# A two-layer kernel with a routed expert stage: expert units of 128 rows in place of 256, four result buffers, one PSUM bank per block, and the transposed rows copied by VectorE

## The reference

```python
P = softmax(xn @ Wg)                       # 8 experts
_, topk_idx = top_k(P, 2)                  # two experts for each token
P_norm = P * mask / (sum(P * mask) + EPS)
h   = gelu(einsum('bsd,edf->ebsf', xn, W1) + b1)   # 128 -> 512
y_e = einsum('ebsf,efd->ebsd', h, W2) + b2         # 512 -> 128
y   = einsum('ebsd,bse->bsd', y_e, P_norm)
x   = x + s * silu(y)
```

## Time and profile before

| | us |
|---|---|
| three runs | 524.37, 519.02, 523.99; median 523.99 |
| profiled execution, its time | 523.02 |
| profiled execution, span of its instructions | 521.3 |

### The profile page before, as it was taken

The page is one execution under the profiler, slowest core; times in us unless marked ns, Lnnn a source line. Parts: engine busy times, 40 slices in busy tenths (PEclk is TensorE's granted clock), DMA queues, the critical chain, the costliest instruction groups (busy, mean ns, idle before and its releaser), DMA issues.

```text
span 521.3 us, 10243 instructions
## 1 busy us (share of the span) xinstructions
PE 460.1 (88%) x3176; PEld 392.3 (75%) x3176; DVE 291.8 (56%) x1056; ACT 215.9 (41%) x528; POOL 165.6 (32%) x251
## 2 busy tenths in 40 slices
PE   3868979999999999999998898999999999999633
PEld 2556867987888978879877687788888888888511
DVE  6687976947785848576666843133233333333327
ACT  3354436453563445432444220244444444444412
POOL 8601002304223151334314140033444444444500
PEclk9996979979999999999998987799999999999958
DMA  7799000000000010000001031011222222222177
GB/s 196 236 269 159 10 1 20 22 1 22 21 17 27 1 36 7 22 22 22 22 6 36 6 109 51 1 52 51 58 67 56 67 61 62 62 62 61 51 262 232
DMA packets 37173, 33.22 MB, mean 64 GB/s; under 512 B 5381, under 2 KB 29833, under 8 KB 37129
## 3 DMA queue, kind: packets, MB, share of 16 engines
q1 hardware_dynamic: 32432, 23.66, 17.9%
q0 software_dynamic: 4352, 8.99, 5.1%
q10 hardware_dynamic: 344, 0.03, 0.0%
HBM read 17.32 MB, written 15.34 MB: 63 GB/s over the span
## 4 chain that ended last, share of the span: by engine, by line
PE 80%; DVE 6%; issue 5%; ACT 5%; DMA 2%; SPq 0%; ACTq 0%; DVEq 0%; POOL 0%; POOLq 0%
PE psA L901 14%; PE psB L914 10%; PE psB L744 6%; PE psB L732 6%; PE psC L846 5%; PE psC L832 5%; PE psD L846 3%; PE psD L832 2%; PE psA L683 2%; PE psA L695 2%; PE psA L690 2%; PE psB L891 2%; PE psC L792 1%; PE psB L734 1%; PE psD L881 1%
## 5 line engine op out<-in xcount | busy, mean ns | idle before, releaser
L594 POOL DMA_INDIRECT routed<-send,slot x64 | 63.0, 985 | 157.7 <-DVE send L1299 54.2
L603 POOL DMA_INDIRECT results<-nat,y_to x72 | 70.2, 975 | 111.7 <-DVE nat L1450 98.2
L901 PE MATMUL psA<-xuT,w_all 128*128 128x256 f32 x288 | 73.7, 399 | 9.7 <-issue 5.9
L914 PE MATMUL psB<-w_all,h1T 128*128 128x128 f32 x576 | 70.4, 275 | 1.4 <-ACT h1T L1093 1.4
L901 PEld LDWEIGHTS psA<-xuT,w_all 128*128 128x128 f32 x288 | 52.7, 193 | 22.5 <-ACT h1T L1093 11.8
L914 PEld LDWEIGHTS psB<-w_all,h1T 128*128 128x128 f32 x576 | 67.1, 192 | 1.6 <-ACT h1T L1093 1.6
L1093 ACT ACTIVATE h1T<-psA,b1T 128x256 f32<-128x256 f32 x144 | 57.1, 474 | 26.4 <-PE psB L914 16.7
L1422 DVE TENSOR_SCALAR xu<-ring 128x256 f32 (+1 forms) x38 | 11.2, 296 | 80.7 <-DMA ring<-routed 54.6
L1084 ACT ACTIVATE xuT<-psB 128x256 f32<-128x256 f32 x37 | 14.2, 383 | 63.1 <-PE psB L891 57.5
L732 PE MATMUL psB<-xnT,w_l 128*128 128x512 f32 x64 | 35.1, 631 | 0.5 <-ACT selT L1012 0.5
L744 PE MATMUL psB<-w_l,hg0T 128*128 128x128 f32 x256 | 32.7, 281 | 0.0
(11 more groups left out here) (244 smaller groups left out, 881.5 us busy)
## 6 DMA issues: line engine op xcount, KB each, us to landing
ring<-routed SPq DMA_DIRECT2D x38, 130.0 KB
w_all<-results SPq DMA_DIRECT2D x16, 256.0 KB, 5.6
routed<-ring SPq DMA_DIRECT2D x24, 130.0 KB, 6.8
w_all<-in_L_ffn_W_dram SPq DMA_DIRECT2D x1, 2048.0 KB, 9.7
out_dram<-x_all SPq DMA_DIRECT2D x8, 256.0 KB, 2.4
results<-nat,y_to POOLq DMA_INDIRECT x72
routed<-fill SPq DMA_DIRECT2D x8, 130.0 KB
routed<-send,slot POOLq DMA_INDIRECT x64
```

What stands on the lines that cost most here:

```text
L594: pool.indirect_dma_start(routed[:, :], bass.IndirectOffsetOnAxis(ap=slot[par][:, c, t:t + 1], axis=0), send[par][:, c, t, :], None).then_ ...
L603: pool.indirect_dma_start(results[:, :], bass.IndirectOffsetOnAxis(ap=y_to[:, par, a:a + 1], axis=0), yw[:, par, a, :], None).then_inc(S[f ...
L901: last = mm(psA[:, j // 2, (j % 2) * UNIT:(j % 2 + 1) * UNIT], w1_all[:, e, j * P:(j + 1) * P], xuT[:, :], start=True, stop=True)
L914: last = mm(psB[:, 1, col(a)], h1T[:, k, a * P:(a + 1) * P], w2_all[:, f * JF + k, :], start=(k == 0), stop=(k == JF - 1))
```

## The change

The unit becomes 128 rows, so each step works on one half only. VectorE instead of ScalarE copies the transposed rows. Four result buffers in place of two, each with a semaphore; GpSimd waits for the send before the last one. Each of the four blocks of the first product has a bank of its own (psA and psC, two banks each) and its own signal. The table's end for the sends is rounded up to a multiple of four. `RING` stays 4, and `MIN_UNITS` 3.

```diff
-HALVES = 2
+HALVES = 1
+SENDS = 4
 UNIT = HALVES * P
 RING = 4
...
-        yw = nat[:, 0:2 * HALVES, :].rearrange("p (i a) d -> p i a d", i=2)
-        yb = nat[:, 2 * HALVES:3 * HALVES, :]
-        y_to = sb("y_to", [P, 2, HALVES], U32)
+        yw = nat[:, 0:SENDS * HALVES, :].rearrange("p (i a) d -> p i a d", i=SENDS)
+        yb = nat[:, SENDS * HALVES:(SENDS + 1) * HALVES, :]
+        y_to = sb("y_to", [P, SENDS, HALVES], U32)
...
+        def hid_ps_of(j):
+            return (psA, psC)[j // 2][:, j % 2, 0:UNIT]
...
-            def send_results(u, par):
-
-                wait_on(pool, "yw_ready", u + 1)
+            def send_results(u, i):
+
+                wait_on(pool, "yw_ready", u + i + 1)
                 pool.sem_inc(apart, 1)
                 for a in range(HALVES):
                     pool.indirect_dma_start(
-                        results[:, :], bass.IndirectOffsetOnAxis(ap=y_to[:, par, a:a + 1], axis=0),
-                        yw[:, par, a, :], None).then_inc(S[f"y_sent{par}"], 16)
-                if not (isinstance(u, int) and u == 0):
-
-                    pool.wait_ge(S[f"y_sent{1 - par}"], (u + par) * (8 * HALVES))
+                        results[:, :], bass.IndirectOffsetOnAxis(ap=y_to[:, i, a:a + 1], axis=0),
+                        yw[:, i, a, :], None).then_inc(S[f"y_sent{i}"], 16)
+                if not (isinstance(u, int) and u + i < 2):
+                    pool.wait_ge(S[f"y_sent{(i + 2) % SENDS}"],
+                                 u * (16 // SENDS * HALVES) + (16 * HALVES if i >= 2 else 0))
                     pool.sem_inc(S["y_landed"], 1)
...
-            with pool.Fori(E, pairs_end, 2) as u:
-                send_results(u, 0)
-                send_results(u + 1, 1)
-            pool.wait_ge(S["y_sent1"], pairs_end * (8 * HALVES))
+            with pool.Fori(E, sends_end, SENDS) as u:
+                for i in range(SENDS):
+                    send_results(u, i)
+            for i in range(SENDS):
+                pool.wait_ge(S[f"y_sent{i}"], sends_end * (16 // SENDS * HALVES))
...
                 pe.wait_ge(S["xuT_ready"], u + 1)
                 for j in range(JF):
-                    if j % 2 == 0:
-
-                        wait_on(pe, "gelu_ready", (u - 1) * JF + j + 2)
-                    last = mm(psA[:, j // 2, (j % 2) * UNIT:(j % 2 + 1) * UNIT],
-                              w1_all[:, e, j * P:(j + 1) * P], xuT[:, :], start=True, stop=True)
-                    if j % 2:
-                        last.then_inc(S["hid_ps"], 1)
+                    wait_on(pe, "gelu_ready", (u - 1) * JF + j + 1)
+                    mm(hid_ps_of(j), w1_all[:, e, j * P:(j + 1) * P], xuT[:, :],
+                       start=True, stop=True).then_inc(S["hid_ps"], 1)
                 turn(u + 1)
...
                     load_bounds(BOUNDS_BY[k])
+                    if k == 0:
+                        wait_on(pe, f"xinvT{JOINS_C}_ready", groups)
                     hid(k, k)
...
-            def turned(u):
-                act.wait_ge(S["xuT_ps"], u + 1)
-                f(xuT[:, :], psB[:, 0, 0:UNIT], ACT.Copy).then_inc(S["xuT_ready"], 1)
-
             def gelus(u, e):
                 for j in range(JF):
                     n = e * JF + j
-                    if j % 2 == 0:
-                        act.wait_ge(S["hid_ps"], u * (JF // 2) + j // 2 + 1)
-
+                    act.wait_ge(S["hid_ps"], u * JF + j + 1)
                     wait_on(act, "h1_free", (u - 1) * JF + j + 1)
-                    f(h1T[:, j, :], psA[:, j // 2, (j % 2) * UNIT:(j % 2 + 1) * UNIT], ACT.Gelu,
+                    f(h1T[:, j, :], hid_ps_of(j), ACT.Gelu,
                       bias=b1T[:, n:n + 1]).then_inc(S["gelu_ready"], 1)
...
+            def turned(u):
+                dve.wait_ge(S["xuT_ps"], u + 1)
+                dve.sem_inc(apart, 1)
+                v.tensor_scalar(xuT[:, :], psB[:, 0, 0:UNIT], 1.0, None, ALU.mult).then_inc(S["xuT_ready"], 1)
+
             def take_ahead(u):
-                dve.wait_ge(S["xuT_ps"], u + 2)
+                turned(u + 1)
                 take(u + 2)
...
-                wait_on(dve, "y_landed", u - 1)
+                wait_on(dve, "y_landed", u + 1 - SENDS)
                 at = ring[:, bass.ds(u % RING, 1), :, :]
-                mine = bass.ds(u % 2, 1)
+                mine = bass.ds(u % SENDS, 1)
```

More of the change, by code:

```diff
@@ L339, in two_block_kernel @@
             "yw_ready",
-            "y_sent0", "y_sent1",
+            *(f"y_sent{i}" for i in range(SENDS)),
             "y_landed",
@@ L343, in two_block_kernel @@
         )}
-        SEEDED = {"yb_ready": 1, "y_landed": 2, "unit_in": 1, "ring_free": RING, "h1_free": JF,
+        SEEDED = {"yb_ready": 1, "y_landed": SENDS, "unit_in": 1, "ring_free": RING, "h1_free": JF,
                   "gelu_ready": JF, "yw_ready": 1}
@@ L357, in packed @@
             return ps[:, 0:TILES * HALF].rearrange("p (t n b) -> p t n b", t=TILES, b=1 << lv)
-        assert J0 == 4 and JOINS_C == 3 and LEVELS == 7 and E == 8
+        assert SENDS == 4 and J0 == 4 and JOINS_C == 3 and LEVELS == 7 and E == 8
         def gate_tiles(p):
@@ L615, in unit_work @@
                 elif what == "out":
-                    send_results(k, k % 2)
+                    send_results(k - k % SENDS, k % SENDS)
             first_pass(pool, work, unit_work)
-            send_results(E - 1, 1)
+            send_results(E - SENDS, SENDS - 1)
             pool.wait_ge(table_ready, 1)
-            pairs_end = pool.value_load(table[0:1, 2 * E + 1:2 * E + 2], min_val=E,
-                                        max_val=MAX_UNITS + 1)
-            with pool.Fori(E, pairs_end, 2) as u:
-                send_results(u, 0)
-                send_results(u + 1, 1)
-            pool.wait_ge(S["y_sent1"], pairs_end * (8 * HALVES))
+            sends_end = pool.value_load(table[0:1, 2 * E + 1:2 * E + 2], min_val=E,
+                                        max_val=MAX_UNITS + SENDS - 1)
+            with pool.Fori(E, sends_end, SENDS) as u:
[3 more added lines that the diff above has]
+                pool.wait_ge(S[f"y_sent{i}"], sends_end * (16 // SENDS * HALVES))
             pool.sem_inc(all_landed, 1)
@@ L915, in out @@
                                   w2_all[:, f * JF + k, :], start=(k == 0), stop=(k == JF - 1))
-                        if a:
+                        if a == HALVES - 1:
                             last.then_inc(S["h1_free"], 1)
@@ L1100, in unit_work @@
             def unit_work(what, k=0):
[L1101 to L1105, removed]
+                if what == "gelu":
                     gelus(0, 0)
@@ L1113, in _ @@
             first_pass(act, work, unit_work)
-            other_units(act, bounds, lambda u, e: turned(u + 1), out)
+            other_units(act, bounds, lambda u, e: None, out)
             for g in range(groups):
@@ L1412, in make_table @@
                                          cnt_f[:, e:e + 1], ALU.add))
-                link(v.tensor_scalar(units_i[:, 0:1], bound_f[:, E:E + 1], 1.0, None, ALU.add))
-                v.tensor_scalar(table[:, 2 * E + 1:2 * E + 2], units_i[:, 0:1], 1, 1,
+                link(v.tensor_scalar(units_i[:, 0:1], bound_f[:, E:E + 1], float(SENDS - 1), None, ALU.add))
+                v.tensor_scalar(table[:, 2 * E + 1:2 * E + 2], units_i[:, 0:1], 2, 2,
                                 ALU.logical_shift_right, ALU.logical_shift_left)
@@ L1456, in unit_work @@
                     take(0)
-                    dve.wait_ge(S["xuT_ps"], 1)
+                    turned(0)
                     take(1)
@@ L1469, in _ @@
             wait_on(dve, "yw_ready", bounds[E])
-            dve.sem_inc(S["yw_ready"], 1)
+            dve.sem_inc(S["yw_ready"], SENDS - 1)
             def finish(g):
```

## The result

The changed kernel takes 574.22 us (median of 4, 573.55 to 579.06) against 522.81 us for the kernel before: ratio 1.10, 95% interval 1.093 to 1.110, slower. The forecast was 572 us with 546 to 600. The profiled execution has a span of 573.0 us and a time of 574.78.

A forecast was written before the change was run, and what follows sets the result against it. The ring loop was to replace TensorE as bound: take 4 at 339.0, 64 turns of 3.0 us, 3.9 and 4.9 us of stalls, 2.3 and 28.1 us to the end, plus 1.7 us around the span: 572 us, range 546 to 600.

The forecast's parts named there:

- the ring loop: Routed expert stage: VectorE's slot release and SyncE's next load wait for each other; 3.50 us before, 3.0 us forecast.
- VectorE's part: Ring loop, from take to weights read: 0.88 us before, forecast 0.67 us at 128 rows, bounds 0.44 and 0.88.
- The way to SyncE: Ring loop, from VectorE's weights read to SyncE's load instruction: 0.24 us, forecast unchanged.
- Issue to take: Ring loop, from SyncE's load instruction to VectorE's next take: 2.38 us before, forecast 1.97, bounds 1.55 and 2.38.
- rival B: Ring loads hardly get shorter, only 0.15 of 2.38 us goes: turn 3.25 us, 588 us in all; chance 0.12.
- Take 4: VectorE's first take that waits for a released ring slot: at 342.16 before, forecast 339.0.
- Last take: VectorE's final take, of 68 in the unit stage, forecast at 539.8 after 64 turns and the stalls.
- the bounds: VectorE's stall while reading the bounds, forecast to add 3.9 us to the ring loop.
- the late takes: Four takes with late loads in the earlier trace, forecast to add 4.9 us to the loop.
- inside TensorE's 0.26 us gap: Where the banks' wait was placed, a gap at each unit that will lie under the ring loop; worth nothing.
- A: Rival: in the unit stage TensorE stays the bound and the padding is saved: 517 us; chance 0.06.
- C: Rival shown by half clock between 340 and 530 us; chance 0.06 in some strength.

The follow-up runs named there:

- ring8: The changed kernel with RING = 8 in place of 4, nothing else; 516.86 us, ratio 0.9956 to the kernel before.
- depth5: The changed kernel with eight ring slots of which only five may be in use; ratio 0.9993 to the kernel before.
- early_free: The changed kernel, RING 4, with VectorE's bias addition moved behind its two ring reads so the slot is released earlier; ratio 1.0941 to the kernel before.
- copy_act: The changed kernel, RING 4, with the copy of the transposed rows back on ScalarE; 576.87 us, ratio 1.1086 to the kernel before.
- before_banks: The kernel before (256 rows, RING 4) with only a bank and a signal for each block of the first product; ratio 0.9766 to the kernel before.
- sends2: The changed kernel with RING = 8, the copy on ScalarE and only two result buffers; ratio 1.0024 to the kernel before.

## Why the prediction was right

**What bounds the stage.** Right: the ring loop, hidden by 0.76 us before, became the bound when TensorE's part halved. It was argued from the waits of both sides and a turn in which VectorE was late; shown by `ring8` and `depth5`, which take the loss away without touching any work, by `early_free`, where the turn follows the release, and by `copy_act`, which moves work without touching the loop and changes nothing. One reading was too simple: the 4.26 us of before were not TensorE's work alone. `before_banks` took 0.37 us off them without any less work, so a wait for ScalarE was part of that turn.

**The loop's terms.** VectorE's part was forecast at 0.67 us and measured 0.81: the two starts that I had shortened for fewer elements stayed as they were for the take (0.21 to 0.20) and fell by 0.04 for the addition (0.36 to 0.32), so instructions of 128 elements cost here nearly what 256 do. The way to SyncE was 0.25 for 0.24. Issue to take was 2.07 for 1.97: halving the rows saved 0.31 us and not 0.4, since the packets' time went from 0.8 to 0.6 us and not to half. The three terms sum to 3.13 us for 2.88 in the turn shown. The turn came to 3.08 us for 3.0, nearer to the forecast than to rival B's 3.25, but in part by luck: I had added 0.1 us for turns in which small VectorE instructions last longer, and what filled it was the shortfall of the terms themselves. Without it the forecast would have been about 564 us.

The page of the Trainium skill that the prediction cites (DMA: Bandwidth & Descriptors, "Anatomy of one DMA") would save 0.15 us, half of the measured 0.31. By its figures the estimate for 65 KB is 2.0 + 0.15 = 2.15 us, close to the measured 2.07, and for 130 KB 2.3, close to 2.38. The section gives them for DMAs that GpSimd issues; these loads are SyncE's, so the closeness is no test of it.

**The sum.** Take 4: 337.87 for 339.0. Last take: 542.14 for 539.8. The 64 turns between them took 204.3 us for 200.8: 64 x 3.08 = 197.1 in place of 192, and 7.2 in place of 8.8 for the bounds and the late takes. The bounds cost 4.9 us for 3.9 (VectorE stood 6.04 us and the turn lasted 8.01), the rest 2.3 for 4.9: only six other turns lasted 3.5 to 3.9 us. From the last take to the end 30.9 us for 30.4. The span is 2.8 us over the forecast's 570.2: 5.1 and 0.5 more, 1.6 and 1.1 less. So errors of opposite sign cancel, and 572 for 574 is closer than the terms are. Of the signs named, TensorE's share is 85% of the span for "about 80%", and VectorE's wait for the load 1.28 us a turn (69.3 / 54) for "near 1.5".

**What I costed at nothing.** The copy on VectorE: right under four slots (`copy_act`). The four result buffers: not taken out under four slots, and about 1% once the loop is open (`sends2`). The banks: no run takes them out of the changed kernel, so that they are worth nothing under the ring loop is argued only. The reason "inside TensorE's 0.26 us gap" hid their worth: at 256 rows they are 2.3%, 0.37 us in each of 36 turns, for the wait for both blocks of a bank was on the path there.

**The rivals.** A's price was 2 to 10 us less than before. `ring8` meets A's condition and comes to a ratio of 0.9956, about 2 us less, the lower end. (That its 516.86 us equals A's 517 is chance: the kernel before had 519.34 us beside it.) The small unit didn't pay even then: the best kernel with 128 rows has 0.9824, those with 256 rows and the banks 0.974 to 0.982. The point of equality, a turn of 2.23 us, is where `depth5` lies: turn 2.22, ratio 0.9993. C: between take 4 and the last take the clock fell twice, each for a little over 3 us. The first time it cost about 0.4 us: eight instructions of L915 took 1.80 us in place of 1.16, VectorE's addition waited 0.39 us for them, and the turn was 3.48 us. The second time the turn was 3.56 us, but by a stop of VectorE before its addition (486.39 to 486.78) that came while the clock was still full; its cause stays open. With stops of about 0.3 us twice in a turn this kernel kept the full clock from 371 to 482 us at 83% busy. That doesn't speak against the section that the prediction names (the Trainium skill, TensorE: Matmul & The Clock Gate, "HAM oscillation"): in its example the products wait for the DMA longer than they compute at every tile, and no run here does that.

## What to carry to other kernels

When work per iteration is halved, list every loop that closes through a DMA: its fixed part doesn't halve, and a loop that hid behind the engine by a fifth of a turn becomes the bound. Look for it in the profile as two queues that wait for each other, and take its length from a turn in which it was late. The cure was one more slot, so that the release used is that of an earlier turn. A bank and a signal for each block was the part of the change that paid, shown with the large unit.

## What was not expected of the hardware

- A VectorE instruction on 128 x 128 f32 from the ring took as long, start to start, as one on 128 x 256: 0.20 and 0.21 us. A read of one word per row straight after the take started 0.40 us later, while an addition from PSUM started 0.20 us after it (`early_free` against the changed kernel). Why isn't settled.
- Loads of 65 KB that SyncE issues one at a time, each when the last has landed, follow each other at 2.15 to 2.3 us (`ring8`), and so seem to cap a stage of 128-row units just above TensorE's 2.05 us.
- Halving the rows of a load from 256 to 128 took its packets' time from 0.8 to 0.6 us and its whole time from issue to take from 2.38 to 2.07 us.
